# The query denominators of a linear-attention and graph kernel: one full-precision product against three products of rounded parts and remainders

## The reference, cut to what matters

```python
phiQ = elu_plus_one(Q)
phiK = elu_plus_one(K)
S = jnp.einsum('bhki,bhkj->bhij', phiK, V)
Z = phiK.sum(axis=-2)
num = jnp.einsum('bhqi,bhij->bhqj', phiQ, S)
denom = jnp.einsum('bhqi,bhi->bhq', phiQ, Z)[..., None] + EPS
context = (num / denom).transpose(0, 2, 1, 3).reshape(B, L, E)
```

## Time and profile before

| | |
|---|---|
| median of 3 runs | 1010.98 us (1010.98 to 1013.32) |
| the profiled execution | 1012.45 us, of which 1010.6 us are the span of its instructions |
| TensorE busy | 986.4 us, 98% of the span |
| VectorE, ScalarE, GpSimd busy | 560.3, 292.6, 143.2 us |
| query stage from 326 to 368 us | TensorE busy 42.00 of 42.00 us, VectorE 31.06, ScalarE 12.39 |
| granted TensorE clock over the span | 0.996 |

### The profile page before, as it was taken

The page is one execution under the profiler, slowest core; times in us unless marked ns, Lnnn a source line. Parts: engine busy times, 40 slices in busy tenths (PEclk is TensorE's granted clock), DMA queues, the critical chain, the costliest instruction groups (busy, mean ns, idle before and its releaser), DMA issues.

```text
span 1010.6 us, 13193 instructions
## 1 busy us (share of the span) xinstructions
PE 986.4 (98%) x4932; PEld 835.3 (83%) x4932; DVE 560.3 (55%) x1033; ACT 292.6 (29%) x564; POOL 143.2 (14%) x192
## 2 busy tenths in 40 slices
PE   4999999999999999999999999999999999999998
PEld 3878888888889988978787688767778999999986
DVE  5886768778754788893112465446655412122354
ACT  5783213214114243241212222113213212135300
POOL 7011001001002023050300000000300203055100
PEclk9999999999999999999999999999999999999999
DMA  7313103013002003122020566445421402010053
GB/s 279 116 50 97 30 17 111 18 32 98 15 28 85 26 26 134 50 70 93 21 86 15 161 190 190 139 146 167 162 88 54 167 1 84 1 42 1 21 186 138
DMA packets 44077, 86.74 MB, mean 86 GB/s; under 512 B 16152, under 2 KB 20612, under 8 KB 43992
## 3 DMA queue, kind: packets, MB, share of 16 engines
q1 hardware_dynamic: 35512, 57.20, 17.3%
q0 software_dynamic: 8480, 28.45, 8.8%
HBM read 61.38 MB, written 23.76 MB: 84 GB/s over the span
## 4 chain that ended last, share of the span: by engine, by line
PE 90%; DVE 6%; ACT 1%; issue 1%; POOL 1%; DMA 1%; DVEq 0%; ACTq 0%; POOLq 0%
PE PS L1405 10%; PE PS L1407 10%; PE PS L1406 10%; PE PS L1511 9%; PE PS L1512 9%; PE PS L1513 9%; PE PS L1569 5%; PE PS L1571 4%; PE PS L1444 3%; PE PS L1588 3%; PE PS L1589 3%; PE PS L1590 3%; PE PS L1640 2%; PE PS L1642 2%; PE PS L1641 2%; PE PS L1420 2%
## 5 line engine op out<-in xcount | busy, mean ns | idle before, releaser
L1405 PE MATMUL PS<-ring,act_t 128*128 128x512 f32 (+1 forms) x480 | 194.6, 405 | 1.7 <-DVE act_t L967 0.9
L1407 PE MATMUL PS<-ring,act_t 128*128 128x512 f32 (+1 forms) x480 | 190.7, 397 | 0.0
L1406 PE MATMUL PS<-ring,act_t 128*128 128x512 f32 (+1 forms) x480 | 190.2, 396 | 0.0
L1511 PE MATMUL PS<-act_t,ring 128*128 128x416 f32 (+1 forms) x432 | 159.3, 369 | 1.4 <-POOL ring L423 1.3
L1512 PE MATMUL PS<-act_t,ring 128*128 128x416 f32 (+1 forms) x432 | 152.1, 352 | 0.0
L1513 PE MATMUL PS<-act_t,ring 128*128 128x416 f32 (+1 forms) x432 | 151.8, 351 | 0.0
L1405 PEld LDWEIGHTS PS<-ring,act_t 128*128 128x128 f32 (+1 forms) x480 | 89.9, 187 | 23.9 <-POOL ring L423 1.6
L1407 PEld LDWEIGHTS PS<-ring,act_t 128*128 128x128 f32 (+1 forms) x480 | 89.5, 186 | 22.4
L1406 PEld LDWEIGHTS PS<-ring,act_t 128*128 128x128 f32 (+1 forms) x480 | 89.8, 187 | 21.4 <-issue 0.5
L1511 PEld LDWEIGHTS PS<-act_t,ring 128*128 128x128 f32 x432 | 81.3, 188 | 6.8 <-issue 3.4
L1512 PEld LDWEIGHTS PS<-act_t,ring 128*128 128x128 f32 x432 | 81.4, 188 | 4.1 <-issue 3.4
(11 more groups left out here) (185 smaller groups left out, 1654.1 us busy)
## 6 DMA issues: line engine op xcount, KB each, us to landing
stage_x<-in_wslices_dram POOLq DMA_DIRECT2D x54, 256.0 KB, 4.2
stage<-in_wslices_dram POOLq DMA_DIRECT2D x42, 256.0 KB, 3.6
xr<-x_d SPq DMA_DIRECT2D x18, 512.0 KB, 3.4
phin_d<-phiq SPq DMA_DIRECT2D x8, 625.0 KB, 3.2
xrow<-in_x_dram SPq DMA_DIRECT2D x9, 512.0 KB, 3.7
xh<-in_x_dram SPq DMA_DIRECT2D x18, 256.0 KB
x_d<-xh SPq DMA_DIRECT2D x18, 256.0 KB
x_d<-xr SPq DMA_DIRECT2D x9, 512.0 KB, 2.7
```

Of the source, the lines that this page charges most:

```text
L1405: pe.matmul(out_ap, node_rows(0, k, t), ring[:, slot(k0 + k), 0, :], start=(k == 0), stop=False)
L1406: pe.matmul(out_ap, node_rows(1, k, t), ring[:, slot(k0 + k), 0, :], start=False, stop=False)
L1407: ins = pe.matmul(out_ap, node_rows(0, k, t), ring[:, slot(k0 + k), 1, :], start=False, stop=(k == KD - 1))
L1511: pe.matmul(out_ap, w[0], x_t[:, 0, k, o:o + n], start=(k == 0), stop=False)
```

## The change

The denominators' product becomes three `F32R` products: rounded key sums times rounded features, rounded key sums times the features' remainder, and the key sums' remainder times rounded features. For that, ScalarE rounds the features into `phi_hl[:, 0]` (`phi_split`) and VectorE makes the remainder in `phi_hl[:, 1]` (`phi_rest`), each once a round; the remainder of the key sums, `z_rem`, is made once by VectorE in round 1 (a clearing of 128x1024, then four subtractions), and the banks of the "z" units are given back by it. TensorE's `denominator` waits for `phi_lo`. Apart from that, TensorE's `extra_counts` test stands one step earlier in the key stage.

```diff
+            z_rem = sb("z_rem", [P, KD, P], F32R, r2)
+            phi_hl = sb("phi_hl", [P, 2, 2, 418], F32R, r2)
...
-            zblk = sb("zblk", [P, KD, P], F32, r3)
+            zblk = sb("zblk", [P, KD, P], F32R, r3)
...
                     nc.scalar.activation(zblk[64:P, 4 * i:4 * i + 4, 64:P], z_ps[64:P, :, 64:P],
-                                         ACT.Copy).then_inc(acc_free[bank(u)], 1)
+                                         ACT.Copy).then_inc(z_hi, 1)
...
+            def phi_split(i):
+                f, c = divmod(i, 3)
+                o, n = CHUNKS[c]
+                act.wait_ge(phiq_ready, i + 1)
+                if i >= 2:
+                    act.wait_ge(den_done, i - 1)
+                nc.scalar.activation(phi_hl[:, 0, i % 2, 0:n], phiq[:, f % PHI_BUFS, o:o + n], ACT.Copy).then_inc(phi_hi, 1)
...
                 if i == 0:
                     sums_out()
+                if i >= 1:
+                    phi_split(i - 1)
                 if i >= 2:
                     den_copy(i - 2)
...
+            phi_split(23)
             act.wait_ge(deg_copied, 1)
...
+            def z_rest(i):
+                u = UNIT["z", i]
+                z_ps = PS[:, bank(u), :].rearrange("p (a b) -> p a b", a=4)
+                for g in range(2):
+                    o = slice(64 * g, 64 * g + 64)
+                    a = slice(4 * i, 4 * i + 4)
+                    ins = dve.tensor_tensor(z_rem[o, a, o], z_ps[o, :, o], zblk[o, a, o].bitcast(F32), ALU.subtract)
+                ins.then_inc(acc_free[bank(u)], 1)
+
+            def phi_rest(i):
+                f, c = divmod(i, 3)
+                o, n = CHUNKS[c]
+                dve.wait_ge(phi_hi, i + 1)
+                dve.tensor_tensor(phi_hl[:, 1, i % 2, 0:n], phiq[:, f % PHI_BUFS, o:o + n],
+                                  phi_hl[:, 0, i % 2, 0:n].bitcast(F32), ALU.subtract).then_inc(phi_lo, 1)
+
             for i in range(24):
                 q_min(i)
+                if i == 1:
+                    dve.wait_ge(z_hi, 2)
+                    link(dve.memset(z_rem[:].bitcast(F32), 0.0))
+                    for j in range(2):
+                        z_rest(j)
+                if i >= 1:
+                    phi_rest(i - 1)
                 if i >= 3:
                     den_invert(i - 3)
                 q_add(i)
...
+            phi_rest(23)
             dve.wait_ge(root_deg, 1)
...
-                pe.wait_ge(phiq_ready, i + 1)
+                pe.wait_ge(phi_lo, i + 1)
                 if i >= 2:
                     pe.wait_ge(den_read, i - 1)
-                pe.matmul(PS[:, 3 + i % 2, 0:n], zblk[:, f, :], phiq[:, f % PHI_BUFS, o:o + n],
-                          start=True, stop=True).then_inc(den_done, 1)
+                for z, b in ((zblk, 0), (zblk, 1), (z_rem, 0)):
+                    ins = pe.matmul(PS[:, 3 + i % 2, 0:n], z[:, f, :], phi_hl[:, b, i % 2, 0:n],
+                                    start=(z is zblk and b == 0), stop=(z is z_rem))
+                ins.then_inc(den_done, 1)
```

More of the change, by code:

```diff
@@ L212, in build @@
         with ExitStack() as r2:
+            sb("pad3", [P, 2 * NT * 512 - KD * P - 4 * 418], F32, r2)
+            z_rem = sb("z_rem", [P, KD, P], F32R, r2)
+            phi_hl = sb("phi_hl", [P, 2, 2, 418], F32R, r2)
+        with ExitStack() as r2:
             hs = sb("hs", [P, 2, NT, 512], F32R, r2)
@@ L302, in build @@
         ex_added = sem("ex_added")
+        z_hi = sem("z_hi")
+        phi_hi = sem("phi_hi")
+        phi_lo = sem("phi_lo")
         qmin_ready = sem("qmin_ready")
@@ L1164, in _ @@
                 dve.wait_ge(ksum_ready, step + 1)
-            dve.memset(zblk[:], 0.0).then_inc(z_cleared, 1)
+            dve.memset(zblk[:].bitcast(F32), 0.0).then_inc(z_cleared, 1)
             dve.wait_ge(small_in, 32)
@@ L1461, in extra_counts, with degree @@
                                 ins.then_inc(ex_used, 1)
-            def degree(dt, more):
-                extra_counts(dt, more)
+            def degree(dt):
                 pe.wait_ge(csum_ready, dt + 1)
@@ L1486, in _ @@
                     window(w)
+                for dt in (tile_ended(step - 2) if step >= 2 else []):
+                    extra_counts(dt, pe_more)
                 for dt in (tile_ended(step - 3) if step >= 3 else []):
-                    degree(dt, pe_more)
+                    degree(dt)
             def key_sums():
```

## The result

| | before | after |
|---|---|---|
| median | 1012.4 us (5 runs) | 1037.65 us (5 runs, 1034.9 to 1038.32) |
| ratio, 95% interval | | 1.0239 [1.0215, 1.0264] |
| profiled execution, span | 1010.6 us | 1035.2 us |
| TensorE, VectorE busy | 986.4, 560.3 us | 993.4, 571.4 us |

The kernel got slower by 2.4%. The span grew by 24.6 us, and 25 were forecast. (With two more runs of the kernel before, its median is 1012.4.)

A forecast was written before the change was run, and what follows sets the result against it. TensorE bounds the kernel before; VectorE was to take over. 2.6 at the start, -0.1, 22.0 over 19 rounds, 0.3 at the weight load and 0.2 behind make 25.0 us, giving a median of 1036 us, range 1029 to 1044.

The forecast's parts named there:

- The step that decides: Query rounds: VectorE's phi_rest waits for ScalarE's Exp, Relu and rounding, making rounds 6.41 us, 1.16 more than before.
- The start: Query stage, round 1: key sums' remainder on VectorE frees the banks late, so q_min(2) comes 2.6 us late.
- The weight load: Rounds 10 and 11: q_add, den_apply and phi_rest stretch beside GpSimd's subtractions, 2.7 us, against 2.4 before.
- TensorE's gain: Query rounds: three products take 0.57 us instead of 0.70, so TensorE's round falls from 5.25 to 5.13.
- what the change could bring at most: All 24 denominators: 3.1 us gained if TensorE still set the pace; not entered in the forecast time.
- Behind the query stage: After q_min(22): h's weight chain 0.5 us later, two denominators give 0.26 back, together 0.2; tail up to 3 in range.
- The moved test: Key stage: extra_counts one step earlier costs nothing, or a fraction of a us ten times if TensorE's cover is gone.
- The signs: Expected in the new profile: VectorE rounds of 6.4 us, waits about 1.7, TensorE idle some 1.3, denominators 0.57 long.
- the granted clock leaves 1.00 in that stage: Query stage: TensorE's clock leaving full level was listed as a sign that the prediction is wrong.
- rival 1: TensorE's clock falls from idling in query rounds: 58 us if it stayed, or about 1049 us; 5% chance.
- Rival 2: Query rounds: VectorE's round still fits, 4.68 under 5.13; 1010.5 us, or 1007.9 without the start's loss; 4% chance.
- Rival 3: Query rounds: only part of the loss appears, 10 to 18 us, about 1025 us; 5% chance.

The follow-up runs named there:

- e1: Changed kernel with phi_rest(i-1) moved behind the reciprocal in VectorE's stream, nothing added or removed: 1015.54 us, 1.004 of the kernel before.
- e2: Changed kernel with phi_split(i-1) moved ahead of Exp(i) in ScalarE's stream, VectorE's order untouched: 1014.53 us, 1.0028 of the kernel before.
- e11: Changed kernel with phi_split(i-1) moved one place further back on ScalarE, behind den_copy(i-2): 1046.24 us, 1.0333 of the kernel before.
- e4: Changed kernel with both repairs, phi_rest behind the reciprocal and the key sums' remainder at the end of round 0: 1012.68 us, 1.0008 of before.
- e6: Changed kernel without phi_rest; the second of the three products takes the rounded features again: 1016.07 us, 1.0033 of the kernel before.
- e8: Kernel before with only the extra_counts test moved one step earlier in the key stage: 1013.3 us, 1.0003 of the kernel before.
- e7: Changed kernel with the one plain 32-bit product instead of three, the split still made but unused: 1035.81 us, 1.0232 of the kernel before.
- e3: Changed kernel with the clearing of z_rem and the four key-sum subtractions moved to the end of VectorE's round 0: 1032.26 us, 1.0217 of before.
- e5: Changed kernel with only the clearing of z_rem moved to the end of round 0, subtractions staying in round 1: 1034.43 us, 1.0211 of before.

## Why the prediction was right

- **The step that decides** held: VectorE waits for a trip through ScalarE that its own `q_min` starts. e1, e2 and e11 show that the wait is the cause, by order alone. Its size was 6.32 instead of 6.41 us: `phi_rest` starts 0.03 behind the rounding's end (356.60 + 0.54 = 357.14, start 357.17), where I had taken 0.11 from the earlier trace rows; I had the 0.03 as the lower bound. The rest of the sum fits to 0.01. Over 19 rounds that is 1.7 us too much.
- **The start** was mis-sized: 2.6 forecast, 4.53 measured, of which 1.5 are the clock (named as a possible fall, not in the sum). The other 0.4: the clearing starts 0.81 behind `q_min` instead of 0.56, and the subtractions stand 1.75 / 4 = 0.44 apart instead of 0.34. The start was 1.9 us too small and the stretch from `q_min(3)` to `q_min(22)` 22.3 - 19.8 = 2.5 too large, and the two nearly cancel. That the sum comes within 0.4 us of the measured 24.6 is luck; the size of the parts carries it only to some 2 us.
- **The weight load**: forecast 2.7 for the first one; the two rounds are 14.56 long (380.25 to 394.81) against 12.64, so 1.9. `q_add` at 1.08 and `phi_rest` at 0.90 were stretched less than I took from the earlier trace rows; `den_apply` at 1.66 was as taken.
- **TensorE's gain** is 5.13 against 5.25 a round, as forecast, where TensorE sets the pace (e1, e2, e4, e6). In the changed kernel it isn't seen, and with both repairs the loads took it back. I had put that as "what the change could bring at most"; the 3.1 us would have been wrong as a forecast for the repaired kernel.
- **Behind the query stage** nothing was added: TensorE went from denominator 22 to the end as before. TensorE's waits from 460 to 520 us name GpSimd's weights (2.3 us) and `phi_rest` once (1.0 us), and no scale factor. The moved test cost nothing (e8).
- **The signs**: two of them came out otherwise. The denominators' products take 0.65 us in the changed kernel (377.00 to 377.65), where they stand behind idle time; in e1, without it, 0.56. And "the granted clock leaves 1.00 in that stage" was named as a sign of being wrong. It did so twice, at the start and at the first weight load:

```profile
384.00:395.00 11.00, 8.28 (x29) 6.18 (x28) 9.45 (x9) 5.06 (x10) 10.27 (x11) 0.80 0.11 32
395.00:405.00 10.00, 10.00 (x48) 9.84 (x48) 6.89 (x8) 3.98 (x8) 4.53 (x6) 0.88 0.69 240
```

The second fall cost nothing that shows: the two rounds there are 1.9 us longer than 2 x 6.32, and the stretched instructions make up 1.9. VectorE sets the pace, so TensorE has time to lose. As a sign it was badly chosen.
- **The rivals**: rival 1 named a falling clock in each or every second round. It fell as told above, and cost 1.5 us instead of 13 to 58. In the undisturbed rounds TensorE's idle time of about 1 us left it at 1.00 (from 336 to 384 us). The 1.4 us a fall in the rival's price had no row behind it; e6 and e7 against the others give 1.4 to 1.5. Rival 2 is what e1 and e2 made come true: at a wait of 0 the round is TensorE's. Their time is not the rival's 1010.5 because of the clock at the start and of the weight loads. Rival 3 did not come: the wait was 1.56 us, near the forecast 1.7.
- **A small misreading**: ScalarE's work in a round is 1.55 us by the earlier trace rows (353.11 to 354.66), where I wrote 1.64. Nothing hangs on it.

## What to carry to other kernels

When work is added to an engine that has idle time, ask what it waits for at its place in the stream, not only how long it takes: here 0.5 us a round was free in one place and cost 1.07 in another, and the same copy on the other engine made the difference from both sides. A wait for something that one's own last instruction has started goes behind the longest instruction that doesn't depend on it, or is started a step earlier. And a gain on the pacing engine arrives at the end only if what paces its next weights moves too. Here the place of one weight rounding was worth 2.4 us in the repaired kernel, and 1.0 in the kernel before.

## What was not expected of the hardware

- Six executions, one each of six kernels, with the same 2.71 us of TensorE idle time gave two outcomes. In four the granted clock went to 0.50 for about 3 us (in the changed kernel, e1 and e2 soon after TensorE had restarted at full clock, in e11 already before it restarted), in two (e6, e7) it stayed at 1.00. The difference is 1.4 to 1.5 us in the time. In single profiles such a thing looks like an effect of the edit. The Trainium skill's "TensorE: Matmul & The Clock Gate", Part 1, says of the rise to full clock that its point varies from run to run. For a fall behind an idle time no run here repeats one kernel's profile, so that it is chance, and not the kernel, is only likely.
- At the first weight load the granted clock left 1.00 in all five kernels in which VectorE sets the pace (the changed one with 0.80 from 384 to 395 us, e3, e5, e7 and e11), and in none of the others. In the changed kernel TensorE waited four times for a weight slice just before, 0.48 to 0.74 us each, from 386.3 to 390.9 us. Up to 390 the clock was 1.00, and from 390 to 394 it was 0.56. In e4 such waits (0.59, 0.58 and 0.74 us in the rows above) left it at 1.00. Why is open.
- Three single-pass products of 416 columns take 0.57 us (0.56 in e1) and not three fourths of 0.70, 0.52. They stand 0.19 apart, and each has a weight load of 128x128 that takes 0.188 us. That it is the load which keeps them apart is only argued: it was not tried by itself.
